# Two-layer cross-attention kernel: the image values of two first-layer units from one set of products, and the last unit's values and quadratic products made one unit later

## The reference, cut to what matters

```python
text, ip = ctx[:, :77], ctx[:, 77:]
q, k, v = hidden @ Wq.T, text @ Wk.T, text @ Wv.T
k_ip, v_ip = ip @ Wk_ip.T, ip @ Wv_ip.T
out = attend(q, k, v) + attend(q, k_ip, v_ip)
x1 = out @ Wo.T + bo + hidden
```

## Time and profile before

| | us |
|---|---|
| three runs, median (lowest, highest) | 769.26 (768.16, 772.94) |
| the profiled execution | 770.42 |
| its span, first to last instruction | 768.5 |
| outside the span | 1.92 |
| busy: PE, DVE, ACT, POOL | 718.9, 571.4, 421.0, 400.3 |

### The profile page before, as it was taken

One profiled execution on the slowest core, in us unless ns is written; L12 is line 12 of the kernel. 1 busy time (PEld: TensorE's weight loads), 2 busy tenths in 40 slices (PEclk: granted clock), 3 DMA queues, 4 the chain that ended last, 5 costly groups with the idle time before them and its releaser, 6 DMA issues.

```text
span 768.5 us, 17327 instructions
## 1 busy us (share of the span) xinstructions
PE 718.9 (94%) x6304; PEld 559.4 (73%) x6304; DVE 571.4 (74%) x1586; ACT 421.0 (55%) x908; POOL 400.3 (52%) x311
## 2 busy tenths in 40 slices
PE   5879799999999999999998999999999999989796
PEld 5767578888787877777776787777777777656474
DVE  5457476868686776968679789697897897875865
ACT  5325445664647475655465655555656555555551
POOL 5512130120203031114488987879869778798763
PEclk9989899999999999999999999999999999999999
DMA  9969843876766683837274164352532732300010
GB/s 278 225 203 238 229 163 104 272 176 213 186 211 169 213 215 101 222 89 203 74 210 133 49 193 142 95 183 73 148 131 74 206 116 76 89 1 31 8 35 18
DMA packets 102339, 111.32 MB, mean 145 GB/s; under 512 B 9928, under 2 KB 99952, under 8 KB 100720
## 3 DMA queue, kind: packets, MB, share of 16 engines
q1 hardware_dynamic: 101904, 109.89, 50.5%
q10 hardware_dynamic: 352, 0.33, 0.2%
HBM read 64.82 MB, written 43.03 MB: 140 GB/s over the span
## 4 chain that ended last, share of the span: by engine, by line
PE 71%; DVE 13%; DMA 6%; issue 4%; POOL 3%; SPq 2%; ACT 1%; POOLq 0%; DVEq 0%; ACTq 0%
PE pB L415 21%; PE pB L590 13%; PE pB L570 4%; PE pB L540 4%; PE pPV L617 4%; PE pB L679 4%; PE pPV L622 4%; PE pPV L612 4%; DVE m_sb L1204 3%; PE pB L575 3%; PE pB L631 3%; PE pPV L608 2%; DVE Y L1220 2%; DMA KP<-k0d 2%; PE pB L469 2%
## 5 line engine op out<-in xcount | busy, mean ns | idle before, releaser
L1466 POOL TENSOR_TENSOR Y<-P,wkv 128x512 f32<-128x512 f32 x160 | 206.0, 1310 | 72.0 <-ACT P L960 71.9
L590 PE MATMUL pB<-wkv 128*128 128x512 f32 x560 | 147.9, 403 | 3.5 <-DVE ipS L1206 3.1
L1204 DVE TENSOR_REDUCE m_sb<-pB 128x2 f32<-128x504 f32 x160 | 106.9, 675 | 30.1 <-PE pB L540 29.8
L1220 DVE TENSOR_TENSOR Y<-pB,Y 128x512 f32<-128x512 f32 x160 | 104.5, 681 | 28.6 <-PE pB L590 22.9
L590 PEld LDWEIGHTS pB<-wkv 128*128 128x128 f32 x560 | 101.5, 189 | 33.1 <-DVE ipS L1206 6.4
L1436 POOL TENSOR_TENSOR klo<-xin,khi 128x256 fp32r<-128x256 f32 x20 | 14.6, 752 | 199.8 <-ACT khi L863 199.8
L950 ACT ACTIVATE wkv<-pB 128x512 fp32r<-128x512 f32 x160 | 86.4, 593 | 49.1 <-PE pB L570 30.4
L960 ACT ACTIVATE P<-pB 128x512 f32<-128x512 f32 x160 | 86.6, 598 | 43.8 <-PE pB L570 29.6
L960 ACT ACTIVATE P<-pB,ln 128x512 f32<-128x512 f32 x160 | 101.4, 694 | 0.0
L863 ACT ACTIVATE Vs<-pPV 128x512 f32<-128x512 f32 (+1 forms) x80 | 39.2, 490 | 106.9 <-PE pPV L622 61.4
L1202 DVE TENSOR_REDUCE m_sb<-pB 128x2 f32<-128x358 f32 x160 | 83.5, 522 | 0.0
(11 more groups left out here) (179 smaller groups left out, 1290.0 us busy)
## 6 DMA issues: line engine op xcount, KB each, us to landing
QP<-q0d SPq DMA_DIRECT2D x64, 192.0 KB, 4.4
KP<-k0d SPq DMA_DIRECT2D x64, 192.0 KB, 4.9
q0d<-qhi SPq DMA_DIRECT2D x32, 256.0 KB, 2.7
k0d<-khi SPq DMA_DIRECT2D x32, 256.0 KB, 2.4
cd<-cc SPq DMA_DIRECT2D x6, 1024.0 KB, 7.9
cc<-cd SPq DMA_DIRECT2D x6, 1024.0 KB, 6.1
c_sb<-in_cT SPq DMA_DIRECT2D x10, 512.0 KB, 5.8
q0d<-qlo SPq DMA_DIRECT2D x16, 256.0 KB, 2.8
```

The lines of the kernel that those rows point to most:

```text
L590: made = mm(bank[:, :], G[i][:, col:col + 128], ph[:, src, :, :].rearrange("p a s -> p (a s)"), start=(n == 0), stop=(n == len(jobs) - 1))
L1204: nc.vector.tensor_reduce(m_sb[:, :, h], v[:, :, 0:TXT1], AX, ALU.max)
L1220: tt(y, bank_of["gp", q, dst][:, :], y, MUL).then_inc(dv_y, 1)
L1466: tt(y, w, r.bitcast(F32), SUB).then_inc(po_y, 1)
```

## The change

Four things change. First, `JOBS` becomes `FIRST_JOBS` and `SECOND_JOBS`: a first-layer unit with an even number has no `V1`; the `V1` of the odd unit after it makes the first-chunk image values of both. For that GpSimd copies tokens 64 to 127 of each unit's context, both planes, into a 128-token tile `two_ctx`, which lies in the space of `VB` (`keep_tokens`, one instruction a unit, 8 in all): the even unit's tokens become rows 64 to 127 of the product, the odd unit's rows 0 to 63. ScalarE then makes two copies and VectorE two clears for the pair, instead of one of each for each unit.

Second, `PACE` for even first-layer units is a row of its own, with 92 products in place of 104. Third, `LAST` sets the pace of units 13 and 14: unit 13 makes only the first four jobs of unit 15 (53 products), and `V1`, `V2`, `G0`, `G1` (36 products) are spread over unit 14. Fourth, waits for the new tile (`po_two`) stand where the context is overwritten and before a `V1`; the load of `VB` waits for the last `V1` of the first layer; `weigh` waits for `dv_fix` by pairs.

```diff
-JOBS = (("Qa", "Qb", "Kt", "Ka", "Kb", "KT", "V0", "V1", "V2"),
-        ("Qa", "Qb", "Ka", "Kb", "V1", "V2", "G0", "G1"))
+FIRST_JOBS = (("Qa", "Qb", "Kt", "Ka", "Kb", "KT", "V0", "V2"),
+              ("Qa", "Qb", "Kt", "Ka", "Kb", "KT", "V0", "V1", "V2"))
+SECOND_JOBS = ("Qa", "Qb", "Ka", "Kb", "V1", "V2", "G0", "G1")
-PACE = ((13, 13, 12, 12, 11, 10, 10, 9, 8, 6), (12, 11, 11, 11, 10, 9, 9, 6, 5, 5))
+PACE = (((12, 12, 11, 11, 10, 9, 8, 7, 7, 5), (13, 13, 12, 12, 11, 10, 10, 9, 8, 6)), (12, 11, 11, 11, 10, 9, 9, 6, 5, 5))
+LAST = ((9, 8, 8, 8, 7, 6, 4, 3, 0, 0), (3, 5, 3, 5, 3, 5, 3, 5, 2, 2))
...
+        two_ctx = VB_all[:, 0:EC * 2 * 128].bitcast(F32R).rearrange("p (k z t) -> p k z t", k=EC, z=2)
...
+                    pairs = [(c, v) for v, c in pairs512(w, slice(0, n), ts)]
+                    if job == "V1" and L == 0:
+                        pe.wait_ge(po_two, u + 1)
+                        pairs = [(two_ctx[:, k, c, :], w[:, v, k, 0:C]) for k in range(EC) for c, v in ((0, 0), (1, 0), (0, 1))]
+                    yield from chain(bank[:, 0:n], pairs, pe_bg, bank)
...
-                    pe.wait_ge(dv_fix, u + 1)
+                    pe.wait_ge(dv_fix, u // 2 + 1)
...
-                for _ in ahead:
-                    pass
+                if u != U - 3:
+                    for _ in ahead:
+                        pass
...
+                    ac.wait_ge(po_two, min(u, B))
...
-                        copy(VYh[i][64:128, 0, :, 0:D], src[64:128]).then_inc(ac_bg, 1)
+                        copy(VYh[(u - 1) % 3][64:128, 0, :, 0:D], src[64:128])
+                        copy(VYh[i][64:128, 0, :, 0:D], src[0:64]).then_inc(ac_bg, 1)
...
+                    nc.vector.memset(VYh[(u - 1) % 3][64:TXT0, 0, :, 0:D], 0.0)
...
+            def keep_tokens(u):
+
+                at = 64 if u % 2 == 0 else 0
+                po.wait_ge(ac_c, 4 * u + 4)
+                po.wait_ge(lo_c, 4 * u + 4)
+                if u >= 2:
+                    po.wait_ge(pe_bg, job_no(u - 1 if u % 2 == 0 else u - 2, "V1"))
+                nc.gpsimd.tensor_copy(two_ctx[:, :, :, at:at + 64], cc[:, :, :, 64:128].bitcast(F32)).then_inc(po_two, 1)
...
+            keep_tokens(0)
             po.wait_ge(lo_w["vi0"], 1)
             nc.gpsimd.memset(QP[1][:, :, :, :].bitcast(F32), 0.0).then_inc(po_set, 1)
...
+            keep_tokens(1)
```

More of the change, by code:

```diff
@@ L49, in lay, with jobs, pace_of @@
     return u // B
+def jobs(u):
+    return SECOND_JOBS if lay(u) else FIRST_JOBS[u % 2]
+def pace_of(u):
+    return PACE[1] if lay(u) else PACE[0][u % 2]
 def job_no(u, job):
-    before = 9 * u if u <= B else 9 * B + 8 * (u - B)
-    return before + JOBS[lay(u)].index(job) + 1
+    before = sum(len(jobs(v)) for v in range(u))
+    return before + jobs(u).index(job) + 1
 def low_no(u, job):
@@ L86, in plan @@
     L, q = lay(u) if u >= 0 else 0, u * NP + j
-    pace = () if u + 2 >= U else FIRST if u < 0 else PACE[lay(u + 2)]
+    ahead = min(u + 2, U - 1)
+    pace = () if u == U - 1 else LAST[u - (U - 3)] if u >= U - 3 else FIRST if u < 0 else pace_of(u + 2)
     pieces = []
     if pace:
-        before = sum(pace[:j])
+        before = sum(pace[:j]) + (sum(LAST[0]) if u == U - 2 else 0)
         for n in thirds(pace[j]):
@@ L93, in plan @@
             done = []
-            for job in JOBS[lay(u + 2)]:
+            for job in jobs(ahead):
                 ends += SIZE[job]
@@ L98, in plan @@
             before += n
-            pieces.append([("bg", n)] + [("done", u + 2, job) for job in done])
+            pieces.append([("bg", n)] + [("done", ahead, job) for job in done])
     else:
@@ L313, in build @@
             sem(f"dv_{n}") for n in ("q", "mx", "bg", "fix", "y", "nb", "o", "n2", "st", "sr", "ot", "op", "bd", "add", "f", "wt", "set", "ip", "vg", "ic"))
-        po_y, po_rn, po_ip, po_set, po_v, po_q, po_mix = (sem(f"po_{n}") for n in ("y", "rn", "ip", "set", "v", "q", "mix"))
+        po_y, po_rn, po_ip, po_set, po_v, po_q, po_mix, po_two = (sem(f"po_{n}") for n in ("y", "rn", "ip", "set", "v", "q", "mix", "two"))
         lo_x, lo_c = sem("lo_x"), sem("lo_c")
@@ L517, in prepare @@
                 for job, ch, w in (("V0", 0, wv), ("V1", 0, wvi), ("V2", 1, wvi))[L:]:
+                    if job not in jobs(u):
+                        continue
                     bank = take("bg", u, job)
@@ L525, in prepare @@
                     n = C + NIP * L
-                    yield from chain(bank[:, 0:n], [(c, v) for v, c in pairs512(w, slice(0, n), ts)], pe_bg, bank)
+                    pairs = [(c, v) for v, c in pairs512(w, slice(0, n), ts)]
[3 more added lines that the diff above has]
+                    yield from chain(bank[:, 0:n], pairs, pe_bg, bank)
                 for ch in range(2 * L):
@@ L755, in tensor_program @@
             for u in range(-1, U):
-                ahead = prepare(u + 2) if u + 2 < U else iter(())
+                ahead = prepare(u + 2) if u + 2 < U else ahead if u == U - 2 else iter(())
                 for j in range(NP):
@@ L1017, in scalar_program @@
                 split_w(wki, ski0[:, ks], (l_w["ki0"], 16), ks)
-            for job in JOBS[0][:2]:
+            for job in jobs(0)[:2]:
                 projection(0, job)
@@ L1021, in scalar_program @@
             split_w(wvi, svi0, (l_w["vi0"], 16))
-            for job in JOBS[0][2:]:
+            for job in jobs(0)[2:]:
                 projection(0, job)
@@ L1523, in gpsimd_program @@
                             split_c(*a)
+                            if a[0] < B:
+                                keep_tokens(*a)
                     if u == 0 and j == 3:
@@ L1598, in load_image_values @@
                 sp.wait_ge(po_mix, u - B)
+                sp.wait_ge(pe_bg, job_no(B - 1, "V1"))
                 dma(VB_all[:, :], vipd[u - B:u - B + 1, :].to_broadcast([128, NIP * C])).then_inc(l_vb, 16)
```

4 lines of the change are left out of this document (2 added, 2 removed).

## The result

The changed kernel took 760.58 us (median) against 768.71 us for the kernel before on the same chip; the ratio of the runs is 0.986, 95% interval 0.982 to 0.991: faster by 1.4%. One of its four executions took 1675.7 us, for which no trace shows a cause: it is in that median, which would be 759.47 us without it, but not in the ratio. The profiled execution took 761.68 us with a span of 759.8 (before 770.42 and 768.5). The forecast was 757.6 us. On a second chip the same comparison gave 0.988 (0.984 to 0.992).

The account below looks back on a forecast made before the run. TensorE was taken as the main bound, 71% of the chain of waits. Unit 0 7.5, units 2 and 4 1.6, units 13 and 14 2.8, copies -0.2: 11.7 us, so 758.7 profiled, 757.6 median; range 754 to 765.5.

Parts of the forecast that it names:

- Unit 0: Step 9's wait for the low row: landing at 86.7 instead of 91.55 gains 4.85, clock staying up 2.6; together 7.5 us.
- (a): Rival: unit 0's low row stays late, key stores ending right ahead of it; 7.5 us missing, 765.1; chance 0.15.
- (b): Rival: unit 0's wait shortens but the clock falls all the same; 2.6 us less, 760.2; chance 0.17.
- The start: Unit 0's V1 set stands ahead of the wait for KP: no gain, TensorE idles 1.8 us longer.
- GpSimd's copies: Eight copies at 0.8 us each, seven in idle time; the first, at the start, costs 0 to 1, taken 0.2.
- Units 2 and 4: 1.8 us of products go from each, 1.0 us of new wait for the low row; 0.8 each, 1.6 us gained.
- the same issue time leaves them as they were: Units 2 and 4: next keys' loads behind the low row in the queue, waiting for the same stores, stay unchanged.
- The price of a set: A set of 12 value products at 0.149 us each is 1.8 us; four sets go.
- rival (d): Slower: the row late in every even unit, units 2 and 4 +2.8 us each; 772.3 us; chance 0.06.
- Unit 13: Steps 4 to 9 become GpSimd-bound at about 27.9 us, gaining 3.1; steps 0 to 3 gain 0.2; 3.3 us.
- Unit 14: Added products mostly hidden in steps 0 to 3; later work about fits if the clock stays up; loss of 0.5 us.
- Rival (c): Unit 14 gives back unit 13's gain, GpSimd waiting there instead; 2.8 us less, 760.4; chance 0.10.

Follow-up runs that it names:

- changed_again: The changed kernel run once more with no edit, beside three variants on one chip: median 761.27 us, ratio 0.988 to the kernel before.
- experiments 1 and 2: Only the two 640 KB loads moved: 1 is loads_early, ratio 0.991 to the kernel before; 2 is loads_late, ratio 1.0005.
- loads_early: Kernel before, with only the two 640 KB weight loads of unit 0 issued ahead of unit 2's key stores: median 764.4 us, ratio 0.991.
- last_only: Kernel before with only the part for unit 15 (new pace of units 13 and 14), first layer as before: ratio 0.998.
- experiment 5: Changed kernel with GpSimd's copy of unit 0's tokens behind the clear of QP and unit 1's low halves: ratio 0.9875 to the kernel before.
- loads_late: Changed kernel with the two 640 KB loads put back behind the key stores in unit 0: median 771.0 us, ratio 1.0005 to the kernel before.
- pairs_only: Changed kernel without the part for unit 15, units 13 and 14 paced as before, first-layer pairing kept: ratio 0.9895 to the kernel before.
- experiment 4: Changed kernel paced so the transposed text keys end in step 5, unit 0's two loads one step earlier: ratio 0.984 to the kernel before.
- keys_copy: Changed kernel with keys ending in step 5, loads one step earlier and GpSimd's start copy late: median 757.61 us, ratio 0.983 to the kernel before.
- experiment 6: Variants moving unit 14's products; the one cited adds unit 15's V1 to unit 13 in keys_copy: 757.22 us, ratio 0.982 to the kernel before.

## Why the prediction was right, and where it was off

The sign and the size class are right: 760.6 lies in the range of 754 to 765.5, 3 us above the forecast. The number is in part luck: units 2 and 4 missed by 3.2 us and unit 15 by 2.3, and 1.7 us that were not forecast came in between units 5 and 13.

**Unit 0, forecast 7.5: right in mechanism and nearly in size.** The row landed by 85.58, where 86.7 was said, TensorE waited 0.86, where 1.3 was said, and the clock stayed at 1.00 behind it. Up to step 7 of unit 1 the changed kernel leads by 8.2 us, near the upper bound of 8.7; from step 7 of unit -1 to there it gains 8.3, and 6.9 in `changed_again`, the second profile of the same code. That the order in the queue does it, and not the smaller number of products, is shown by experiments 1 and 2. Rivals (a) and (b) did not happen in unit 0. Experiment 2 shows what the loads do once they stand behind the stores: 7.63 us of wait. The windows behind the waits show the clock: 1.00 behind 0.86 us, 0.58 behind 4.60. The rule of the Trainium skill in "HAM oscillation — how this bites in real kernels" ("TensorE: Matmul & The Clock Gate") names waits for transfers as what throws the clock back: by these two it agrees for the long wait, and the short one was harmless. Waits of a length between these two were followed by either clock, as units 2 and 4 show below.

**The start, forecast 0: right as far as the runs can tell.** In the changed kernel's profile the maxima start at 29.65 in place of 30.58; the first load of `KP` is issued at 24.49, before at 25.80. But its clock is 0.59 and 0.56 from 30 to 34 us, where it was 1.00 before, and step 7 of unit -1 stands at 47.84 against 47.75. Over the other profiles with the pairing the maxima start between 29.44 and 30.75, without it (`loads_early`, `last_only`) at 30.54 and 30.76. A gain of up to 1 us is neither shown nor excluded. The longer idle time was there: 1.53 us for `klo`, where the kernel before has none.

**GpSimd's copies, forecast 0.8 us each and 0.2 in all: 0.61 each, cost not measurable (experiment 5).** The Trainium skill's 769 ns for a tight loop over 512 elements ("GPSIMD Engine Reference", section "3.1 Elementwise — side-by-side cycle accounting") is 0.16 above the trace.

**Units 2 and 4, forecast 1.6: wrong, they lost about 1.6.** The row was issued when it was said to be: 155.74 is 3.3 us behind step 7 of unit 2, and the forecast (163.1, with step 7 some 1.2 us before 161.32) has it 3.0 behind. It was waited for as said in unit 2 (1.02 us; 0.42 in unit 4). That wait lies in the window of 35.68 us, not in the one of 33.89 ahead of it, so from step 7 of unit 1 to step 7 of unit 3 nothing was gained: 69.57 us in place of 69.22.

The step that failed is "the same issue time leaves them as they were", on the next keys. Two things took their time away. The loads wait 0.7 and 0.8 us in SP's queue for the last of the stores, which now end right ahead of them; and TensorE, with twelve products fewer, comes to the keys sooner. In unit 4 of the kernel before the loads are issued at 233.69, 5.8 us ahead of the maxima that use them (239.48); in the changed kernel at 226.83, 4.4 us ahead of TensorE's arrival (231.21), and the keys have landed only at 232.74, a wait of 1.53. How long the loads take counts too: here the keys land 5.9 us after the issue, but in `loads_late` and `pairs_only`, with the same order in unit 4, after 4.5, and TensorE waits only 0.27 and 0.22. Why stays open. With the keys back in step 5 all of this is gone (experiment 4), and `keys_copy` is 3.7 us under `changed_again` by the medians.

The price of a set was too high as well. Where nothing waits, in the four profiles with the keys in step 5, two sets fewer make the stretch from step 7 of unit 1 to step 7 of unit 5 2.7 to 2.9 us shorter, so 1.4 a set and not 1.8.

The stretch differs from profile to profile: the same code in it takes 140.7 to 141.8 us in four other profiles and 138.43 in `loads_late`, against 139.98 here and 138.4 in all three without the pairing. The price that rival (d) names, a wait near 2 us and a slow stretch, is seen in unit 2 of `pairs_only`, though the stores came as worked out:

```profile
159.74 0.73 PE L592 MATMUL pB<-QP,KP 116*128 116x512 f32 x2 [1.93 <-DMA QP<-mlo]
```

```profile
160.00:162.00 2.00, 2.00 (x15) 1.25 (x18) 0.38 (x1) 1.70 (x4) 0.10 (x1) 0.72 0.99 256
162.00:164.00 2.00, 2.00 (x21) 0.59 (x13) 0.00 (x0) 1.04 (x4) 1.79 (x3) 0.50 1.13 207
```

In all, seven waits of 1.53 to 1.93 us for the row or the keys stand in units 2 and 4 of these six profiles. Behind four of them (1.56, 1.59, 1.70, 1.93) the clock of the next 3 us was 0.53 to 0.69; behind three (1.53, 1.62, 1.81) it was 1.00. So rival (b) was right about the danger and wrong about the place.

**Unit 13, forecast 3.3: 2.7.** Split where the earlier trace rows splits it, at the first scores of step 4:

```profile
599.17:620.62 21.45, 19.51 (x175) 14.35 (x171) 19.13 (x54) 10.82 (x21) 14.92 (x12) 1.00 0.38 127
620.62:648.37 27.75, 26.48 (x232) 20.04 (x228) 21.92 (x50) 16.85 (x36) 26.29 (x18) 1.00 0.39 116
```

Steps 4 to 9 lasted 27.75 us, near the 27.9 of the forecast, though neither engine alone is the bound: GpSimd is idle for 1.5 us and TensorE for 1.3. What is missing is in steps 0 to 3, 21.45 us in place of 20.89 where 0.2 less was said. Step 3 lasts 6.68 us, before 5.66; TensorE waits 0.85 us in it for VectorE's product, and VectorE works without a gap from 611.71 until that product is done. That fits the forecast's reading that VectorE sets these steps; why its work on step 3's product ends later, and so why the 0.2 didn't come, was not tested. Twelve more products in steps 4 to 9 cost 0.6 (experiment 6).

**Unit 14, forecast -0.5: right in the number, wrong in what it is made of.** The number compares two profiles, and unit 14 was 1.7 us longer in that of before (47.63, clock 0.93) than with the same code in `loads_early` (45.94, clock 1.00). "It followed a wait of 1.90 us for the image mix" was read as cause; `loads_early` has a wait of 2.2 us at that place and no slow stretch behind it. Measured against `loads_early`, the products cost 1.75: 0.8 in steps 0 to 3 (21.04 us, there 20.23), where they were called hidden and put at 0.2, and 0.95 in steps 4 to 9 (26.66, there 25.71). Rival (c)'s result is mostly what happened: of the 2.8 forecast for units 13 and 14, 0.95 is the change's. Its mechanism, that GpSimd waits in unit 14 for what it doesn't wait for in unit 13, was not tested.

**Unit 15, forecast 0: -2.3 in the profile.** The code is the same. TensorE is busy 52.33 us for the same 394 matmuls in place of 49.54. The clearest piece is the last output products (line 709; 691 before), four of which take 1.06 us in place of 0.63:

```profile
752.20 1.06 PE L709 MATMUL pB<-ahi,wo 128*128 128x256 f32 x4
```

```profile
761.48 0.63 PE L691 MATMUL pB<-ahi,wo 128*128 128x256 f32 x4
```

No experiment ties this to the change: unit 15 took 60.77 to 63.73 us in the ten profiles with the part for it (mean 62.2), and 61.48, 61.51 and 62.73 in the three without (mean 61.9). What decides in which waits of units 14 and 15 the clock falls stays open.

## What to carry to other kernels

Before pricing a pace by its products, list which queue entries it moves past each other: here one digit that moved two big loads ahead of a small, awaited row was worth two thirds of a rewrite, and the same rewrite with the digit the other way was worth nothing. When products are taken out between a load and its consumer, a load whose issue "stays" has become late by what was taken out, and it may now have to wait for a store that used to be long done, so each consumer's slack has to be read again. And a half-clock stretch next to a wait in one profile is no price of that place: read the same code in a second profile before counting its loss as something to win back.

## What was not expected of the hardware

A small row behind two loads of 640 KB in one queue landed 7.3, 7.6 (`last_only`) and 8.2 us after its issue. Where they were not right ahead of it, TensorE waited for the row 18 times in units 0, 2 and 4 of the profiles; it landed 1.7 to 2.1 us after its issue in 17 of them and 2.5 us in one. Waits of TensorE between 1.53 and 1.93 us were followed by a clock of 0.53 to 0.69 in four cases of seven and by full clock in the other three. Unit 15, whose code no edit touched, took 60.8 us (clock 1.00) to 63.7 us (clock 0.95), a spread wider than what most of the edits tried here gave.
